# Expert layer of a two-layer perceiver: blocks gathered by token number, gated outputs added straight to the output rows

## The reference, cut to what matters

```python
normed = (xt - mu) * rsqrt(var + 1e-5) * ln_gamma + ln_beta      # 1024 x 256
probs = softmax(normed @ router_w.T)                             # 8 experts
top_v, top_i = top_k(probs, 2)
gates = softmax(top_v)
comb = sum(one_hot(top_i, 8) * gates[..., None], axis=1)
for e in range(8):
    y = _swiglu(normed, gate_up_w[e], down_w[e])                 # 256 -> 2 x 768 -> 256
    out = out + comb[:, e, None] * y
out = out + _swiglu(normed, shared_gate_up_w, shared_down_w)     # 256 -> 2 x 256 -> 256
x = x + out
```

## Time and profile before

| | |
|---|---|
| median of 3 runs | 2050.94 us (2046.54 to 2051.79) |
| the profiled execution: device time | 2052.2 us |
| the profiled execution: span | 2050.2 us |
| TensorE busy (matmul) | 1851.5 us, 90% of the span |
| VectorE, ScalarE, GpSimd busy | 63%, 46%, 41% |
| start of the expert layer's normalisation in the span | about 1764.7 us |
| end of the last block's copy to `yS` | 2023.35 us |

### The profile page before, as it was taken

The page is one execution under the profiler, slowest core; times in us unless marked ns, Lnnn a source line. Parts: engine busy times, 40 slices in busy tenths (PEclk is TensorE's granted clock), DMA queues, the critical chain, the costliest instruction groups (busy, mean ns, idle before and its releaser), DMA issues.

```text
span 2050.2 us, 43679 instructions
## 1 busy us (share of the span) xinstructions
PE 1851.5 (90%) x17650; PEld 1559.1 (76%) x17650; DVE 1290.4 (63%) x2731; ACT 941.1 (46%) x2016; POOL 841.1 (41%) x922
## 2 busy tenths in 40 slices
PE   5999999999998589668999999999999899689994
PEld 4788888778887478568999999989999756446662
DVE  4788888888888565445666766667666536522222
ACT  4766676666665233524444444444444234112220
POOL 4777777777775340205333333333332013130002
PEclk9999999999999689878999999999999989789997
DMA  6121121112101100122322223222221060311102
GB/s 201 35 66 35 34 66 35 34 47 54 34 3 54 42 1 2 49 80 60 89 57 57 57 57 101 69 57 57 57 68 46 20 265 2 123 59 31 32 29 72
DMA packets 55655, 119.78 MB, mean 58 GB/s; under 512 B 4433, under 2 KB 41889, under 8 KB 53921
## 3 DMA queue, kind: packets, MB, share of 16 engines
q1 hardware_dynamic: 53920, 112.80, 18.6%
q0 software_dynamic: 1536, 4.20, 0.6%
HBM read 107.80 MB, written 9.18 MB: 57 GB/s over the span
## 4 chain that ended last, share of the span: by engine, by line
PE 72%; DVE 9%; ACT 6%; issue 6%; DMA 3%; POOL 1%; SPq 0%; POOLq 0%; DVEq 0%; ACTq 0%
PE ps L163 7%; PE ps L104 7%; PE ps L2158 6%; PE ps L480 5%; PE ps L462 4%; PE ps L1366 4%; PE ps L439 3%; DMA wsb<-in_ctxT 3%; PE ps L2182 3%; PE ps L1367 3%; PE ps L456 2%; PE ps L390 2%; PE ps L1352 2%; PE ps L1351 2%; PE ps L1355 2%
## 5 line engine op out<-in xcount | busy, mean ns | idle before, releaser
L537 DVE TENSOR_REDUCE arena<-ps 128x1 f32<-128x400 f32 (+1 forms) x512 | 257.7, 566 | 95.2 <-PE ps L439 95.2
L668 ACT ACTIVATE arena<-ps 128x384 f32<-128x384 f32 (+1 forms) x512 | 223.4, 523 | 102.7 <-PE ps L462 102.7
L1366 PE MATMUL ps<-arenaR 128*128 128x386 f32 x768 | 246.6, 356 | 1.1 <-DVE arenaR L1453 1.1
L740 POOL TENSOR_TENSOR arena<-arena 128x512 f32<-128x512 f32 (+1 forms) x160 | 208.4, 1303 | 89.7 <-ACT arena L668 80.9
L1552 ACT CAST arenaR<-ps 128x512 fp32r<-128x512 f32 (+1 forms) x256 | 116.7, 508 | 226.1 <-PE ps L163 226.1
L1367 PE MATMUL ps<-arenaR 128*128 128x256 f32 x768 | 215.7, 281 | 0.0
L1595 POOL TENSOR_TENSOR arenaR<-h,arenaR 128x400 fp32r<-128x400 f32 (+1 forms) x60 | 57.9, 966 | 375.0 <-ACT arenaR L1537 375.0
L1453 DVE TENSOR_TENSOR arenaR<-ps,arenaR 128x512 fp32r<-128x512 f32 (+1 forms) x256 | 138.9, 584 | 25.4 <-ACT arenaR L1552 24.8
L1435 DVE TENSOR_TENSOR arenaR<-wsb,arenaR 64x400 fp32r<-64x400 f32 x64 | 66.2, 1039 | 139.0 <-ACT arenaR L1538 139.0
L1366 PEld LDWEIGHTS ps<-arenaR 128*128 128x128 f32 x768 | 145.4, 189 | 1.3 <-DVE arenaR L1453 1.3
L1367 PEld LDWEIGHTS ps<-arenaR 128*128 128x128 f32 x768 | 146.4, 191 | 0.0
(11 more groups left out here) (319 smaller groups left out, 4710.8 us busy)
## 6 DMA issues: line engine op xcount, KB each, us to landing
wsb<-in_ctx SPq DMA_DIRECT2D x16, 1152.0 KB
arena<-in_ctxT SPq DMA_DIRECT2D x16, 800.5 KB, 5.3
arena<-in_ctxT SPq DMA_DIRECT2D x32, 400.2 KB, 7.3
wsb<-in_ctxT SPq DMA_DIRECT2D x32, 400.2 KB, 7.4
gu<-in_m_gu SPq DMA_DIRECT2D x8, 1536.0 KB, 20.5
h<-in_ctxT SPq DMA_DIRECT2D x15, 800.5 KB, 5.1
dn<-in_m_dn SPq DMA_DIRECT2D x8, 768.0 KB, 9.3
xs_rows<-zeros SPq DMA_DIRECT2D x1, 2944.0 KB, 15.8
```

What stands on the lines that cost most here:

```text
L537: e.tensor_reduce(mx4[n % 2][:, u, i:i + 1], ps[:, at("look", n, i, u), 0:400 + (i == 3)], AX.X, ALU.max).then_inc(c.maxed.at((n, i, u)), 1)
L668: e.activation(v[:, u, 0:128 * GN[s]], ps[:, at("st", n, s, u), 0:128 * GN[s]], ACT.Exp).then_inc(c.exp_a.at((x0, n, s, u)), 1)
L740: e.tensor_tensor(acc_p[0:k], acc_p[0:k], v[0:k, :, 128 * t:128 * t + 128], ALU.add).then_inc(added_p.at((n, s)), 1)
L1366: e.matmul(o, PTh[:, t, :], v[:, t, 0:386], start=(t == 0), stop=False)
```

## The change

The table of rows and the copies in DRAM are replaced by a small table that says, for each row p of each block i, which token it is and with what gate.

- **Table by products.** VectorE works with `pos` in units of blocks. It compares `pos` of all 16 x 128 entries with 0 to 22 (`C_`), takes differences (`ce`, one-hot over the blocks), sums for the block number (`blk`), and compares the rest with 0 to 127 in 128ths (`rows`, one-hot over the rows in a block, two instructions of 128 x 1024). `B` holds `ce` times the token's number plus one and, by a GpSimd instruction, `ce` times its gate. 16 products of `rows` with `B` (46 columns), summed in PSUM bank 7, give the table: numbers and gates. From it come `ids` (whole numbers; rows without a token get 1024 + p) and `gate`. The gates are made earlier, ahead of the wait for the ranks.
- **Order.** The shared expert uses other PSUM banks, so that `shared_gu(1, 0)` can run early. TensorE's order becomes: logits, `shared_gu(0, 0)`, ranks, `shared_gu(0, 1)`, `shared_gu(1, 0)`, table, `shared_down(0)`, `shared_gu(1, 1)`, `shared_down(1)`, blocks. VectorE's `shared_act` comes behind the table.
- **Gather.** SyncE stores `h` once to `h_rows` in DRAM (1024 rows and 128 of zeros). GpSimd gathers each block by `ids` (`gather(i)`). The 16 scatters and the 23 loads go.
- **Add to the output.** SyncE stores `x` with the shared part added to the output in two halves. `down` on VectorE multiplies by the gate while it copies to `yS`. GpSimd adds `yS` to the output's rows by an indirect DMA with an add (`add(i)`), each behind the one before; rows above 1023 are dropped. The 23 stores to `ys_rows`, the 16 gathers at the end, the 16 gate instructions and the three output stores go.
- **Zeros.** The 2944 KB write of zeros at the start becomes two of 128 KB.

The core of the diff:

```diff
@@ sp
-        def load_block(i):
-            w.wait_ge(*scattered(15))
-            ...
-            e.dma_start(xs[i % 3], c.xs_d[128 * i:128 * i + 128, :]).then_inc(in_xs[i % 3].at(i, 16), 16)
-        def store_y(i):
-            w.wait_ge(*y_out(i))
-            e.dma_start(c.ys_d[128 * i:128 * i + 128, :], yS[i % 2]).then_inc(out_ys[i % 2].at(i, 16), 16)
...
+        w.wait_ge(*c.normed((mo, NT - 1)))
+        w.wait_ge(*c.zeroed("rows"))
+        e.dma_start(c.xs_d[0:1024, :].rearrange("(t p) c -> p t c", p=128), c.h[:, :, :]).then_inc(h_out.at("h", 16), 16)
+        for half in range(2):
+            w.wait_ge(*c.x_new((mo, "shared", 4 * half + 3)))
+            e.dma_start(rows_out[512 * half:512 * half + 512, :].rearrange("(t p) c -> p t c", p=128),
+                        x[:, 4 * half:4 * half + 4, :]).then_inc(sum_out.at(half, 16), 16)
+        w.wait_ge(*added(NS - 1))
@@ pe
+        def table(k):
+            w.wait_ge(*routing(("rows", k)))
+            w.wait_ge(*routing("numbers"))
+            w.wait_ge(*gated("in"))
+            for t in range(NT):
+                p = e.matmul(ps[:, 7, 0:2 * NS], rows[:, 8 * k + t, :], B[:, 8 * k + t, :], start=(k == 0 and t == 0), stop=(k == 1 and t == NT - 1))
+            if k:
+                p.then_inc(routed.at("table"), 1)
...
-        for f in range(2):
-            shared_gu(0, f)
+        shared_gu(0, 0)
         w.wait_ge(*routing("chosen"))
         e.matmul(ps[:, 7, 0:64], tri, flat(M), start=True, stop=True)
         e.matmul(ps[:, 7, 64:128], ones, flat(M), start=True, stop=True).then_inc(routed.at("ranks"), 1)
+        shared_gu(0, 1)
+        shared_gu(1, 0)
+        w.wait_ge(*routing("placed"))
+        for k in range(2):
+            table(k)
         shared_down(0)
-        for f in range(2):
-            shared_gu(1, f)
+        shared_gu(1, 1)
         shared_down(1)
@@ dve, behind pos
+        e.tensor_tensor(C_[:, :, 0:NS], pos.unsqueeze(2).broadcast_to([128, 16, NS]), iota.unsqueeze(1).broadcast_to([128, 16, NS]),
+                        ALU.is_ge).then_inc(c.dv.at(), 1)
...
+        e.tensor_tensor(ce, C_[:, :, 0:NS], C_[:, :, 1:NS + 1], ALU.subtract).then_inc(routing.at("placed"), 1)
+        e.tensor_reduce(blk, C_[:, :, 1:NS + 1], AX.X, ALU.add).then_inc(c.dv.at(), 1)
...
+        e.tensor_tensor(row, pos, blk, ALU.subtract).then_inc(c.dv.at(), 1)
...
+        for k in range(2):
+            u = slice(8 * k, 8 * k + 8)
+            e.tensor_tensor(rows[:, u, :], row128.unsqueeze(1).broadcast_to([128, NT, 128]), row[:, u].unsqueeze(2).broadcast_to([128, NT, 128]),
+                            ALU.is_equal).then_inc(routing.at(("rows", k)), 1)
+            if k == 0:
+                w.wait_ge(*routing("placed"))
+                for i in range(2):
+                    v = slice(8 * i, 8 * i + 8)
+                    e.tensor_tensor(B[:, v, 0:NS], ce[:, v, :], number.unsqueeze(2).broadcast_to([128, NT, NS]),
+                                    ALU.mult).then_inc(routing.at("numbers"), 1)
...
+        w.wait_ge(*routed("table"))
+        e.tensor_scalar(empty, ps[:, 7, 0:NS], 0.0, spare, ALU.is_equal, ALU.mult).then_inc(c.dv.at(), 1)
+        w.wait_ge(*c.dv.now())
+        e.scalar_tensor_tensor(ids, ps[:, 7, 0:NS], -1.0, empty, ALU.add, ALU.add).then_inc(routing.at("ids"), 1)
+        e.tensor_copy(gate, ps[:, 7, NS:2 * NS]).then_inc(routing.at("gates"), 1)
@@ dve, down(i)
             if i >= 2:
-                w.wait_ge(*out_ys[i % 2](i - 2))
-            e.tensor_copy(yS[i % 2], ps[:, (5, 7)[i % 2], 0:256]).then_inc(y_out.at(i), 1)
+                w.wait_ge(*added(i - 2))
+            e.tensor_scalar(yS[i % 2], ps[:, (5, 7)[i % 2], 0:256], gate[:, i:i + 1], None, ALU.mult).then_inc(y_out.at(i), 1)
@@ pool
+        def gather(i):
+            w.wait_ge(*routing("ids"))
+            w.wait_ge(*h_out("h"))
+            if i >= 3:
+                w.wait_ge(*b_turned(i - 3))
+            e.indirect_dma_start(xs[i % 3], None, c.xs_d, bass.IndirectOffsetOnAxis(ap=ids[:, i:i + 1].bitcast(U32), axis=0)
+                                 ).then_inc(in_xs[i % 3].at(i, 16), 16)
+        def add(i):
+            w.wait_ge(*y_out(i))
+            w.wait_ge(*sum_out(1))
+            if i:
+                w.wait_ge(*added(i - 1))
+            e.indirect_dma_start(rows_out, bass.IndirectOffsetOnAxis(ap=ids[:, i:i + 1].bitcast(U32), axis=0), yS[i % 2], None,
+                                 bounds_check=1023, oob_is_err=False, compute_op=ALU.add).then_inc(added.at(i, 16), 16)
...
+        e.tensor_tensor(B[:, :, NS:2 * NS], ce, g12.unsqueeze(2).broadcast_to([128, 16, NS]), ALU.mult).then_inc(gated.at("in"), 1)
+        for i in range(3):
+            gather(i)
+        for i in range(NS):
+            if i + 3 < NS:
+                gather(i + 3)
+            add(i)
```

More of the change, by code:

```diff
@@ L363, in sp @@
         w.wait_ge(*c.po("zeros"))
-        e.dma_start(c.xs_d.rearrange("(i p) c -> p i c", p=128),
-                    c.zeros[:, :].unsqueeze(1).broadcast_to([128, NS, D])).then_inc(c.zeroed.at("xs", 16), 16)
+        for v in (c.xs_d, c.ys_d):
+            e.dma_start(v[1024:1152, :], c.zeros[:, :]).then_inc(c.zeroed.at("rows", 16), 16)
         for b in range(2, NB):
@@ L2060, in moe @@
     sT, sgs = ar2(128, 2, 512), [ar2(128, 512) for _ in range(2)]
+    rows = ar2(128, 16, 128)
     a_, aT = [ar(128, 768) for _ in range(2)], [ar(128, 6, 128) for _ in range(2)]
@@ L2289, in dve @@
         e.tensor_tensor(M, oh1, oh2, ALU.add).then_inc(routing.at("chosen"), 1)
+        e.tensor_tensor(v2, v2, v1, ALU.subtract).then_inc(routing.at("gap"), 1)
         R = ps[:, 7, 0:64].rearrange("p (t e) -> p t e", e=8)
@@ L2293, in dve @@
         c3 = cmp_[:, 0:64].rearrange("p (a b) -> p a b", b=8)
+        w.wait_ge(*prob("gate"))
+        e.tensor_scalar(g1, g2, 1.0, None, ALU.add).then_inc(c.dv.at(), 1)
+        w.wait_ge(*c.dv.now())
+        e.reciprocal(g1, g1).then_inc(c.dv.at(), 1)
+        w.wait_ge(*c.dv.now())
+        e.tensor_tensor(g2, g2, g1, ALU.mult).then_inc(c.dv.at("gates"), 1)
         w.wait_ge(*routed("ranks"))
@@ L2330, in dve @@
         e.tensor_scalar(itd, texp[0:1, :], 7.0, 1536.0, ALU.min, ALU.mult).then_inc(routing.at("down"), 1)
-        e.tensor_tensor(v2, v2, v1, ALU.subtract).then_inc(routing.at("gap"), 1)
-        w.wait_ge(*prob("gate"))
-        e.tensor_scalar(g1, g2, 1.0, None, ALU.add).then_inc(c.dv.at(), 1)
+        w.wait_ge(*routed("table"))
+        e.tensor_scalar(empty, ps[:, 7, 0:NS], 0.0, spare, ALU.is_equal, ALU.mult).then_inc(c.dv.at(), 1)
         w.wait_ge(*c.dv.now())
-        e.reciprocal(g1, g1).then_inc(c.dv.at(), 1)
-        w.wait_ge(*c.dv.now())
-        e.tensor_tensor(g2, g2, g1, ALU.mult).then_inc(c.dv.at("gates"), 1)
-        for half in range(2):
-            for f in range(2):
-                shared_act(half, f)
-            shared_down(half)
+        e.scalar_tensor_tensor(ids, ps[:, 7, 0:NS], -1.0, empty, ALU.add, ALU.add).then_inc(routing.at("ids"), 1)
+        e.tensor_copy(gate, ps[:, 7, NS:2 * NS]).then_inc(routing.at("gates"), 1)
+        for f in range(2):
+            shared_act(0, f)
+        shared_down(0)
+        for f in range(2):
+            shared_act(1, f)
+        shared_down(1)
         take_block(0)
@@ L2351, in dve @@
         down(NS - 1)
-        w.wait_ge(*c.dv("gates"))
-        w.wait_ge(*c.x_new((mo, "shared", NT - 1)))
-        for t in range(NT):
-            w.wait_ge(*in_yg[t](1))
-            e.scalar_tensor_tensor(x[:, t, :], yg[t], g1[:, t:t + 1], x[:, t, :], ALU.mult, ALU.add).then_inc(c.dv.at(), 1)
-            w.wait_ge(*c.dv.now())
-            e.scalar_tensor_tensor(x[:, t, :], yg[8 + t], g2[:, t:t + 1], x[:, t, :], ALU.mult, ALU.add).then_inc(c.x_new.at((mo, t)), 1)
     def act(e, w):
```

105 lines of the change are left out of this document (46 added, 59 removed).

## The result

The changed kernel takes 2026.07 us in the median of 4 runs (2023.26 to 2026.7), against 2049.49 us of the kernel before in the same comparison (4 runs): ratio 0.9884, 95% interval 0.9867 to 0.9901. The forecast was 2025.8 us. The profiled execution took 2025.8 us and has a span of 2023.4 us, 2.4 us less than its time, where the prediction had left 2.0.

A forecast was written before the change was run, and what follows sets the result against it. TensorE, busy 90% of the span, bounds the block loop; it idles in front and tail. Span 2050.2 - 22.5 (tail) - 2.6 (front) = 2025.1 us; median 2050.94 - 25.1 = 2025.8 us, range 2018 to 2036.

The forecast's parts named there:

- The tail: From the last copy to `yS` to the span's end: 26.85 us becomes 4.3 (2.5 to 5.5), 22.5 us less.
- two bounds by rows: Landing time of an adding DMA of 128 rows: 2.4 us from below (scatter), 5.1 from above (gather plus scatter).
- The rate rule: An add in the DMA engine runs at about half a copy's rate: add 4.8 us, tail 5.1, sum 0.8 worse.
- The loop: Block loop, bound by TensorE at 8.61 us per block: indirect DMAs and VectorE's multiply stay hidden, change 0.
- The rival of slow adds: Chained adds become the loop's bound once an add and its start exceed 8.61 us; 2108 us at period 12; chance 0.07.
- its formula: Loss if adds bind with period P: 22 x (P - 8.61) plus a tail longer by P - 4.3.
- The trap of descriptors that wait for VectorE: GpSimd can't write DMA descriptors while VectorE runs certain fast SBUF-to-SBUF copies; given no price of its own.
- The front: Routing and shared expert ahead of the blocks: `turn_block(0)` 2.6 us earlier; bounds 7.4 less to 5.9 longer.
- the clock stays low: Rival: TensorE's clock low from the table to the blocks, front 5.9 us longer than before, 2034.3 us; chance 0.10.
- the scatters were hardly the bound: Front, first block's load: TensorE waited only 1.06 us for it before; the shared expert was the bound.
- The start: Write of zeros at the kernel's start, 2944 KB taking 15.8 us: gain 0, with 1.5 us less as the bound.

The follow-up runs named there:

- plain_write: Changed kernel with its 23 indirect DMAs to the output as plain writes instead of adds; 2025.61 us, ratio 0.9885 to the kernel before.
- three_adds: Changed kernel with every block's add made three times, each with a third of the gate and behind the one before; 2147.16 us, ratio 1.0478.
- after_again: Changed kernel, unchanged, measured once more for a comparison on one chip; 2027.21 us, ratio 0.9886 to the kernel before.
- order_only: Kernel before with only the new order of the shared expert's products, its PSUM banks and the earlier gates; scatters, loads, stores and gathers kept; ratio 0.9995.
- zeros_back: Changed kernel with the 2944 KB write of zeros put back at the start, into a DRAM tensor nothing reads; ratio 0.989 to the kernel before.
- before: The kernel before the change, with scatters, block loads and the gathers at the end; 2049.49 us median of 4 runs.
- no_last_add: Changed kernel without the adding DMA of the last block, which moves no rows here; 2019.52 us, ratio 0.9852 to the kernel before.
- after: The changed kernel itself, with the whole change; 2026.07 us median of 4 runs, ratio 0.9884 to the kernel before.
- acts_first: Changed kernel with VectorE making half 0's two shared activations before it waits for the table; 2021.91 us, ratio 0.9863 to the kernel before.
- table_late: Changed kernel with four shared down products and the last up part ahead of the table's products; 2017.99 us, ratio 0.9859 to the kernel before.

## Why the prediction was right, point by point

**The tail** was forecast to shrink by 22.5 us and shrank by 20.4, to 6.4 instead of 4.3 us. That is outside the 2.5 to 5.5 us that the prediction gave and also named as a sign, and the path was another than forecast: the prediction had the program end when the last add lands, and it ends with GpSimd's drain. An adding DMA was sized well: 3.8 us to landing in the median against the 4.0 assumed, between the two bounds by rows. But the last one, the only one in the tail, has no rows and landed in 2.7 us; by the forecast's own path the tail would have been 0.8 + 2.7 = 3.5 us. The rate rule of the Trainium skill (Collectives: The Full Stack, The bandwidth ceiling) gave 4.8; `plain_write` (2.5) and the add (3.8) have a ratio of 1.5, so its direction was right and doubling the whole copy too much. GpSimd took 0.8 us (2016.98 to 2017.77) to start on the last add where I had 0.3, its drain runs until 3.8 us after its last indirect DMA's instruction, that instruction is 1.55 us long, and the span ends 0.2 to 0.3 us behind the drain, so the tail is 0.8 + 1.55 + 3.8 + 0.25 us. Before, the drain was hidden behind the last output store, which is why I had not seen it:

```profile
L2426 POOLq DRAIN  x1: 18141/18141/18141, 2030.3 to 2030.3; - x1
```

It ended at 2030.3 + 18.1 = 2048.4, 3.2 us after the last gather's instruction, and the span at 2050.2.

**The loop** cost nothing, as forecast: 201.72 against 201.80 us. The gathers were in time, GpSimd idled 5.75 us of 8.6, and VectorE's multiply took 0.48 instead of 0.42 us, covered. An add occupies GpSimd for 1.59 us, not for the 0.97 of a scatter that the prediction took; that was covered as well. The rival of slow adds is settled by `three_adds`: an add and its start are 4.6 us, so the chain would bind only if each were nearly twice as long. Its price was right in size: with a period of 13.67 us its formula gives 22 x (13.67 - 8.61) + 13.67 - 4.3 = 121 us, and 121 were measured, though divided otherwise (101 in the blocks and 18 in the tail, by the marks of the profile). Its mechanism was right in part: TensorE waits for gathers queued behind the adds, and runs at a lower clock behind the waits. The trap of descriptors that wait for VectorE (the Trainium skill, SBUF — State Buffer, SBUF: two separate sides) did not show: all gathers but the first took 0.94 to 1.02 us on GpSimd, adds 1.55 to 1.62.

**The front** was forecast 2.6 us shorter and was 3.85 (3.9 in `after_again`). Its steps: ranks 3.4 us earlier, measured 4.93 - 1.55 = 3.4. The 128 x 1024 compare 1.22 us, measured 1.22. The table 9.6 to 14.0 us after the choice, measured 1792.05 and 1795.8 less 1782.35: 9.7 and 13.4, since the product instructions cost 0.12 rather than 0.14 us each. `shared_down(0)` at the low clock, right, though for 5.98 us instead of 6.5 and not in the form "the clock stays low": it rose within it, as before. `shared_down(1)` took 3.6 us up to the first block's transposes, not 4.3: the gap ahead of its last tile did not come again; what made it I can't say. The step from the transposes to the first expert product took 3.1 us (1812.16 to 1815.26) where I had left the 2.35 of before. From the forecast's 2.6 us these make the measured 3.85: 0.6 (table), 0.2 (the gap behind it), 0.5 and 0.8 (down products) come on top, and 0.75 (the last step) and 0.1 (`shared_gu(1, 1)`, 3.6 instead of 3.5) come off. That the scatters were hardly the bound was right for the old order, and `order_only` adds what the prediction had not worked out: with the new order they would have been, by 10.29 us, and the front would still have been 3.1 us shorter.

**The start**: 0 was forecast, and `zeros_back` shows none, within the spread of 5 us of the layer's start; the 1.5 us that the prediction gave as a bound are too small for it to exclude. That the median of 2026.07 lies 0.3 us from the forecast is partly luck: the tail's 2.1 us too little are in part made up by 1.25 in the front, and the kernel before has 2049.49 us in this comparison where the forecast started from 2050.94. So the gain is 23.4 us, against a forecast of 25.1.

**What stays open**: what the drain's length follows. It ended 3.1 to 3.2 us after the last indirect DMA's instruction in the two kernels with 32 of them (`before`, `order_only`), 3.7 with 45 (`no_last_add`), 3.8 with 46 (`after`, and `plain_write` too) and 5.1 with 92 (`three_adds`). It rises with their number in these runs, but no run varies the number alone. Open are also the fall of the clock, as said, and why the earlier layers vary by 5 us.

## What to carry to other kernels

A chain of gather, combine and store behind the last product costs its whole length; adding the results to the output from inside the loop hides it, as long as the adds of a block (here 4.6 us of 8.6) end within the time of a block. What ends the program then is no longer the chain of data, so look at the closing instructions of each engine too. When an order is changed, ask of each part alone what comes last then: here the new order without the table gains 3 us and hits the scatters, the table without the new order loses 6, and both together gain 4. Work with slack, like this table, belongs where its operands have long been ready, so that TensorE idles neither ahead of it nor behind it: the same products in such a place gained 7 us in the front and 9 in all.

## What the runs showed of the hardware

- An indirect add of 128 rows of 1 KB from SBUF to DRAM lands 3.8 us after its start (median of 23 in `after`) and occupies GpSimd for 1.55 to 1.62 us; the plain write 2.5 and 1.02 us; the gather 2.8 and 0.99 us. An add or a plain write whose rows are all dropped still lands only after 2.7 and 2.1 us. Chained adds start 4.6 us apart (`three_adds`).
- At the end of these programs GpSimd's drain lasted until 3.7 to 3.8 us after the end of its last indirect DMA's instruction (2019.32 to 2023.1; 2015.70 to 2019.4; in `plain_write` 2016.36 to 2020.2), 2.6 us and more after that DMA had landed. It was 3.2 us in the kernel before and 5.1 in `three_adds`, so 3.8 us is no constant.
- 32 float32 product instructions of 46 columns take 3.74 us at the granted clock of 0.99 (2.4 GHz) and 7.03 us after 8.2 us of idling. The clock was full through such a table behind dense products and 1.3 us of idling and fell at its end, also without a gap behind it (`acts_first`); with dense products and no gap on either side (`table_late`) it stayed full.
